# A decoder layer's causal self-attention: the weighted sum of a block issued in one step instead of four

## What is computed

```python
q, k, v = (split_heads(norm(x) @ W + b) for W, b in ((Wq, bq), (Wk, bk), (Wv, bv)))
scores = einsum('bhid,bhjd->bhij', q, k)
bias = take_along_axis(einsum('bhid,pd->bhip', q, rel_key), clip(j - i + p - 1, 0, p - 1))
attn = softmax(where(j <= i, (scores + bias) * hd ** -0.5, -inf))
x = x + (einsum('bhij,bhjd->bhid', attn, v)) @ Wo + bo
x = x + cross_attention(norm(x), ctx)
x = x + experts(norm(x))
```

## Time and profile before

| | |
|---|---|
| median of 3 runs | 566.52 us (565.25 to 566.54) |
| the profiled execution | 568.64 us, its span 566.8 us |
| TensorE matmul busy | 481.0 us (85%) |
| VectorE busy | 371.7 us (66%) |
| ScalarE busy | 242.1 us (43%) |
| GpSimd busy | 207.2 us (37%) |
| L1167, the weighted sum | 1,280 matmul records |
| L1252, the row sums | 64 matmul records |

### The profile page before, as it was taken

How to read it: one execution, slowest core, us unless ns; L and a number is a source line. 1 busy time by engine, 2 the same in 40 slices (tenths; PEclk the granted TensorE clock), 3 DMA queues, 4 the chain that set the end, 5 groups by cost and what they waited for, 6 DMA issues and landing times.

```text
span 566.8 us, 17578 instructions
## 1 busy us (share of the span) xinstructions
PE 481.0 (85%) x7360; PEld 272.1 (48%) x7360; DVE 371.7 (66%) x759; ACT 242.1 (43%) x738; POOL 207.2 (37%) x125
## 2 busy tenths in 40 slices
PE   0869999999999899999899975886899958868777
PEld 0444655656556465565555642332333325546555
DVE  4866786568856888577885755244246354788785
ACT  0225566555565565665646611233153522313221
POOL 6227493224423834039350082115000003545333
PEclk9889999999999999999999976698798988999898
DMA  8201000000000010000000000000000000000000
GB/s 273 75 37 41 22 3 20 24 21 23 22 2 22 16 27 22 1 23 3 21 3 2 3 2 0 1 1 1 0 2 1 1 0 0 20 0 19 0 19 20
DMA packets 14967, 11.23 MB, mean 20 GB/s; under 512 B 1339, under 2 KB 14127, under 8 KB 14767
## 3 DMA queue, kind: packets, MB, share of 16 engines
q1 hardware_dynamic: 14895, 10.18, 5.8%
HBM read 8.01 MB, written 2.10 MB: 18 GB/s over the span
## 4 chain that ended last, share of the span: by engine, by line
PE 63%; DVE 21%; issue 6%; ACT 5%; POOL 4%; DMA 1%; POOLq 0%; DVEq 0%; SPq 0%; ACTq 0%
PE psT L1227 12%; PE psS L1198 12%; PE psO L1167 7%; PE psS L1208 7%; PE psT L1543 4%; DVE neg_max L897 4%; PE psS L1413 3%; ACT prob L572 3%; PE psS L1418 3%; PE psS L1531 2%; POOL stat L362 2%; PE psT L1387 2%; PE psM L1431 2%; DVE x_max L950 2%; PE psO L1436 2%
## 5 line engine op out<-in xcount | busy, mean ns | idle before, releaser
L572 ACT ACTIVATE prob<-psS,neg_max 128x208 f32<-128x208 f32 (+23 forms) x256 | 121.9, 481 | 119.9 <-DVE neg_max L897 119.6
L362 POOL TENSOR_TENSOR stat<-stat,pack_a_sb 128x4 f32<-128x4 f32 (+2 forms) x17 | 64.8, 3810 | 191.4 <-DVE stat L746 114.2
L897 DVE TENSOR_REDUCE neg_max<-psS 128x2 f32<-128x672 f32 (+23 forms) x128 | 91.9, 718 | 61.6 <-PE psS L1208 59.2
L1227 PE MATMUL psT<-pack_a_sb,prob 128*128 128x128 f32 (+4 forms) x640 | 101.3, 284 | 9.4 <-ACT pt_diag L533 5.3
L1198 PE MATMUL psS<-kT,q_blk 64*32 64x336 f32 (+23 forms) x2048 | 87.9, 400 | 2.8 <-ACT prob L572 1.6
L1227 PEld LDWEIGHTS psT<-pack_a_sb,prob 128*128 128x128 f32 (+4 forms) x640 | 63.0, 132 | 56.4 <-issue 28.5
L1208 PE MATMUL psS<-rel_shifted,q_rel 36*32 36x268 f32 (+16 forms) x2048 | 71.1, 335 | 0.0
L476 POOL TENSOR_TENSOR prob<-prob 128x512 f32<-128x512 f32 x36 | 39.2, 1096 | 67.3 <-ACT prob L674 46.7
L394 POOL TENSOR_TENSOR q_blk<-qT,pack_a_sb 128x1024 f32<-128x1024 f32 x16 | 31.5, 1966 | 86.3 <-PE psS L1208 78.5
L1543 PEld LDWEIGHTS psT<-pack_b_sb,prob 128*128 128x128 f32 x288 | 37.6, 199 | 34.3 <-issue 22.4
L1543 PE MATMUL psT<-pack_b_sb,prob 128*128 128x128 f32 x288 | 40.5, 288 | 15.7 <-DVE X L1091 10.7
(11 more groups left out here) (163 smaller groups left out, 635.4 us busy)
## 6 DMA issues: line engine op xcount, KB each, us to landing
q_rep<-q_scratch SPq DMA_DIRECT2D x128, 32.0 KB
pack_b_sb<-pack_b_dram SPq DMA_DIRECT2D x1, 1859.0 KB, 10.4
X<-x_dram SPq DMA_DIRECT2D x4, 256.0 KB, 5.5
q_scratch<-qT SPq DMA_DIRECT2D x4, 256.0 KB, 2.0
out_dram<-X SPq DMA_DIRECT2D x4, 256.0 KB, 2.3
pack_a_sb<-pack_a_dram SPq DMA_DIRECT2D x1, 535.0 KB, 4.5
pt_even<-ctx_dram SPq DMA_DIRECT2D x1, 154.0 KB
rel_shifted<-rel_base_dram SPq DMA_DIRECT2D x1, 152.0 KB, 5.3
```

What stands on the lines that cost most here:

```text
L362: nc.gpsimd.tensor_tensor(st[:, 5, 0:groups], st[:, 2, 0:groups], ca["root"][0:parts, 0:groups], ALU.pow).then_inc(seeded, 1)
L572: ins = nc.scalar.activation(prob[:, s % 4, half, 0:wide], psS[:, 2 * (s % 2) + half, 0:wide], ACT.Exp, bias=neg_max[:, s % 2, half:half + 1],
L897: v.tensor_reduce(neg_max[:, s % 2], psS[:, 2 * (s % 2):2 * (s % 2) + 2, 0:wide], AX_X, ALU.max, negate=True).then_inc(max_ready, 1)
L1227: ins = nc.tensor.transpose(psT[0:w, k % 2, at:at + T], prob[:, s % 4, half, j * T:j * T + w], ident)
```

## The change

The four quarters of `attend_block` move from steps 2, 3, 4 and 5 into step 4, directly behind one another. `sum_rows` moves from behind the quarter of step 4 to directly in front of the first quarter. Its two products with 64 columns of `row_head` each become four with 32 columns, which write the same values to the same rows of `psM`: they now have the tile shape of the weighted sum, 128 by 32.

```diff
@@ sum_rows
                 pe.wait_ge(spread_ready, k + 1)
                 pe.wait_ge(y_added, k + ONE)
-                for half in range(2):
-                    ins = mm(psM[HALF_ROWS * half:HALF_ROWS * (half + 1), 0:T], ca["row_head"], spread2[:, half, :],
+
+                for q in range(HQ):
+                    half, at = divmod(32 * q, HALF_ROWS)
+                    ins = mm(psM[32 * q:32 * q + 32, 0:T], ca["row_head"][:, at:at + 32], spread2[:, half, :],
                              start=True, stop=True)
                 ins.then_inc(sums_ready, 1)
@@ the loop over steps
                 if s >= 2:
                     transpose_weights(s - 2)
-                if g and 2 <= u <= 5:
-                    attend_block(g - 1, u - 2)
                 b, n = divmod(g, TB)
+                if g and u == 4:
+                    pe.wait_ge(piece_read, pieces_until(g, u))
+                    sum_rows(g - 1)
+                    for i in range(HQ):
+                        attend_block(g - 1, i)
                 f = b - 1
...
-                if g and u == 4:
-                    pe.wait_ge(piece_read, pieces_until(g, u))
-                    sum_rows(g - 1)
```

## The result

| | before | changed |
|---|---|---|
| median | 566.33 us (6 runs, 565.25 to 567.12) | 574.95 us (6 runs, 571.27 to 577.64) |
| ratio | 1 | 1.0152, 95% interval 1.0112 to 1.0192 |
| profiled execution, span | 568.64 us, 566.8 us | 577.03 us, 575.2 us |
| first to last scores of self-attention | 42.44 to 327.98, 285.5 us | 42.85 to 336.86, 294.0 us |

The forecast was 572.8 us, +6.3 on the median, with a range of 568.5 to 577.0. The median moved by +8.6. In the two profiles the span grew by 8.4 us, and the stretch from the first to the last scores of self-attention by 8.5: the whole loss lies there. Four executions among all those of this document (735, 765, 1,095 and 2,366 us) fell far outside the others of their kernels and are in no ratio and in none of the medians given here.

The account below looks back on a forecast made before the run. TensorE was taken to bound self-attention, with the chain over VectorE and ScalarE a near second limit. Terms: 4.9 + 0 + 0.5 + 2.4 - 0.2 - 0.7 - 0.6 = +6.3 us on 566.5, giving 572.8 us, range 568.5 to 577.

Parts of the forecast that it names:

- The price of a quarter and of the joined piece: TensorE: 0.0275 us a record plus 0.13 per quarter for tile shape; joined with row sums 3.87, 2.99 or 2.11 us.
- n = 1: Blocks with three tiles of keys: +0.34 us each in g5, g9, g13, g1 gains 0.54; together +0.5.
- n = 2: Blocks with two tiles of keys: only step 3's removed quarter gains, step 4 grows by 1.17; +0.60 us a block, +2.4.
- n = 0: Blocks with one tile of keys: g8 and g12 bound by the refinement behind GpSimd, cost 0; g4 -0.2 us.
- The third rival: Worse than the sum: refinements slide under GpSimd's passes, up to 2.5 us in each of two blocks; 578 us, chance 0.10.
- n = 3: Blocks with four tiles of keys, g7, g11, g15: -0.75 + 2.49 - 0.10 = +1.64 us a block, +4.9 for three.
- g3: Block with four tiles of keys but no head norm: between -0.54 and +1.64 us, taken as 0.
- the waits taken in: TensorE's existing waits in self-attention that vanish where a new wait just before takes them in: -0.6 us.
- The end of self-attention: Last block's row sums: the chain starts earlier without g15 step 5's quarter, with smaller tiles; -0.7 us, bounds -0.15 and -1.15.
- The first rival: The price of the tile shapes decides, TensorE bounding every step: 8.1 us gained, 558.4 us; chance 0.06.
- The second: Rival: half of the waits don't come, or the tile-shape price exceeds 0.13; 565.6 us, counted 565 to 568.2; chance 0.12.
- sign (2): TensorE's waits in self-attention grow from 10 to about 24 us, some 1.4 before step 4's scores in g7, g11, g15.

Follow-up runs that it names:

- the spreading moved: Changed kernel with VectorE's spreading of the row sums behind the maxima of step 2, not in front; 570.28 us, ratio 1.006.
- the waits of n = 3 filled: Changed kernel plus five products of 128 by 128 that nobody reads, in step 3 of g7, g11 and g15; 574.15 us, ratio 1.0147.
- the last placed version: Row sums as changed; quarters joined in step 5 (n = 0 from g4), halves in steps 2 and 5 (n = 2 from g6), others unmoved; 563.81 us.
- the placed version: Row sums as changed; quarters all in step 5 (n = 0), halves in steps 2 and 5 (n = 2) or 3 and 5 (others); 563.22 us, again 562.01.
- the extra products in all four blocks: Changed kernel plus five products of 128 by 128 that nobody reads, in step 3 of g3, g7, g11 and g15; 575.13 us, ratio 1.0149.

## Why the prediction was right, and what it mis-sized

**The price of a quarter and of the joined piece: right.** Row sums and weighted sum together took 3.85 us in g11 (3.87 foretold), 2.97 in g9 (2.99), and 2.11 in g6, 159.01 to 161.12 (2.11). The row sums' 8 records take 0.24 (214.90 to 215.14), for 0.22. The experiment with them alone shows their 0.15 us to the hundredth.

**n = 1: right.** Foretold +0.5 over four blocks; g1 -0.52, g5, g9 and g13 +0.28, +0.32 and +0.31: +0.4.

**n = 2: right in kind, a bit high.** Foretold +0.60 a block; +0.58, +0.38, +0.24, +0.38. The quarter of step 2 gave nothing: the second transposes of step 3 start 5.2 us behind the scores of step 2 in both kernels, and wait for ScalarE longer than before. The quarter of step 3 gave more than its 0.57: from those transposes to the scores of step 4 it was 1.80 us in g6 and is 1.03.

```profile
155.58 0.66 PE L1227 MATMUL psT<-pack_a_sb,prob 128*128 128x128 f32 x4 [0.59 <-ACT pt_diag L533]
```

**n = 0: cost at nothing, was 0.2 to 0.3** in g8 and g12; in g4 -0.1, for -0.2. The refinement again ends when GpSimd's `q_rel` does; it now starts under `q_blk` and is held twice (compare). `q_rel` ends 13.6 us behind the start of g8 and not 13.4, which is the loss. The third rival feared this sliding at up to 2.5 us a block; it came, and cost a tenth of that. In g8:

```profile
196.63 1.25 DVE L712 SCALAR_TENSOR_TENSOR stat<-stat 128x64 f32<-128x64 f32 x1
...
197.76 2.56 POOL L404 TENSOR_TENSOR q_rel<-q_rep,pack_a_sb 128x1024 f32<-128x1024 f32 x1
197.92 2.49 DVE L713 TENSOR_TENSOR stat<-stat 128x64 f32<-128x64 f32 x1
```

**n = 3: the mechanism right, g3 mis-sized.** g11 took +1.0 and g15, counted to its last scores, +1.2, for the +1.64 of the prediction; g7 without the clock took +1.4, and exactly that in the third profile, where the clock didn't fall in it. g11's number is 0.4 low by a wait that only the profile of the kernel before has. Scores of step 5 to scores of the next block got 0.23 shorter in g7 (3.70 us), not 0.10, since VectorE's maxima no longer wait a little for the scores; the waits taken in at the start of the block, which I had booked apart (-0.6), are in these numbers too (-0.10 a block). g3 was +0.9 in the first profile and +0.4 and +0.6 in the others. g7 was +3.0 in the first, and of this 1.6 is the clock.

**The end of self-attention: right.** The -0.7 was to come from the chain behind g15 step 5 and the smaller tiles. From the scores of that step to the first scores of cross-attention it is 21.55 us before (325.24 to 346.79) and 20.82 after (334.92 to 355.74), 0.73 less; the prediction has 0.10 + 0.7. The larger part of it already lies before the last scores, in the +1.2 of g15: from the last scores on it is 18.8 before and 18.9 after, and the wait for VectorE's spreading is 2.18 in both.

**The step that was missing** is the price of the clock. The prediction named a fall of the granted clock in this stage as something that would make it wrong, and gave it no time. In the first profile it is a term of +1.6. **The term that was mis-sized most** is g3, put at nothing between bounds of -0.54 and +1.64, which took +0.9.

**The sum by position**, to the first scores of cross-attention, first profile: n = 3 with the end and the waits taken in +3.6 without the clock (foretold 4.9 - 0.7 - 0.6 = 3.6), g3 +0.9 (0), n = 1 +0.4 (+0.5), n = 2 +1.6 (+2.4), n = 0 +0.4 (-0.2). Together that is 6.9, and 8.5 with the clock, beside the 6.3 of the prediction. So n = 2 and, against it, g3 and n = 0 were off by 0.6 to 0.9 each and nearly cancel, which is luck; and since single runs scatter by 6 us and the three profiles by 1.3 in this stage, that 8.5 meets the measured 8.6 so closely is luck too.

The first rival, that the price of the tile shapes decides, is refuted by the joined quarters alone. That the change does gain this price is shown by the same timelines; it is hidden below cover that is lost. The second, that half of the waits don't come, is refuted by their sum, which grew by 12 us where sign (2) has 14. The rule of the Trainium skill (TensorEngine Tiling (Array Packing), PSUM Bottleneck) had the direction right, though the time went further than to no change: the waits that grew are those for ScalarE's and VectorE's emptying of `psT` and for the exponentials read out of `psS`. They came because the quarters that covered them were moved, of which the rule says nothing.

## What to carry to other kernels

Before joining pieces of work to save what lies between them, ask what each piece covers where it stands: here a piece in a wait was free, and cost its full time elsewhere. Although the bound engine was 95% busy here, the chain of the others was only tenths of a microsecond shorter than its step, and what precedes the chain's first instruction on its own engine (here 0.67 us of row sums in front of the maxima) counted as much as the bound engine's work. A gain that needs no cover, as the row sums' tile shape (some 2 to 3 us), can be taken alone. Placing the quarters with regard to the waits turned a loss of 8.6 us into a gain of 4, of which some 1 to 2 us goes beyond the row sums. Where a block got shorter by a placing, look at what the other engines did in it before crediting the placing: in g8 it was GpSimd's earlier pass.

## What the runs showed of the hardware that was not expected

The granted clock fell to half for 3.4 us in the middle of a stage in which TensorE is busy for nine tenths of the time. From the first to the last scores of self-attention this happened twelve times, in eight of the fourteen profiles: once in each of the three of the changed kernel, three times with the joined quarters alone, twice with the spreading moved (201.6 and 276.7 us), twice with n = 3 alone, once with the waits of n = 3 filled (201.1) and once in the last placed version (270.6). Each fall began at the end of a single wait of TensorE of 1.3 to 1.9 us, or up to 1.5 us behind it. The kernel before, whose longest wait in g1 to g14 is 1.22, has none; the row sums alone (waits up to 1.37) and the placed version (up to 0.9) have none in two profiles each. But most such waits had no fall behind them: the wait of 1.29 us before the scores of step 4 stands fifteen times in the five profiles that have it, and four falls followed; with the extra products in all four blocks two waits of 1.90 stayed, and no fall followed. What decides it is open.

In two joined pieces of 128 records, g3 and g15 of the first profile, a gap of about 0.3 us appears near the end, though the profile names nothing that they wait for. In g15 it is inside the first row, where 23 records take 1.10 us and 24 take 0.84 elsewhere:

```profile
333.57 1.10 PE L1167 MATMUL psO<-pt_even,V_now 128*32 128x128 f32 x23
334.40 0.37 PE L1167 MATMUL psO<-pt_diag,V_now 128*32 128x128 f32 x3
334.50 0.27 PE L1167 MATMUL psO<-pt_even,V_now 128*32 128x128 f32 x1
334.51 0.48 PE L1167 MATMUL psO<-pt_diag,V_now 128*32 128x128 f32 x5
334.92 0.40 PE L1198 MATMUL psS<-kT,q_blk 64*32 64x96 f32 x16
```

The weighted sum of g15 takes 3.97 us here and 3.6 in the other two profiles of the kernel. Steps of the same length above the rest occur in other profiles too (g15 step 4 with n = 3 alone took 5.04 us for 4.64, g3 step 4 took 5.0 to 5.6). The cause was not tried and stays open.
